# First attention's output projection as 24 products of high and low parts, with new orders of work on all engines

## The reference, cut to what matters

```python
x = x + attn(cond(x, cond_512, ...), norm_g, norm_b, Wq, Wkv, q_scale, k_scale, null_kv, Wout)
x = x + ffn(cond2(x, cond_512, ...), signatures_raw, knot_values, ..., norm_gamma, norm_beta, output_scale)

# in attn, for each sequence (n = 64, h = 16, dh = 64; two null keys in front)
out = jnp.einsum('bhij,bhjd->bhid', softmax(q @ k.T * 8 + bias), v)   # 64 x 1024 a sequence
out = out.transpose(0, 2, 1, 3).reshape(b, n, h * dh)
return out @ Wout                                                     # 1024 x 256
```

## Time and profile before

| | |
|---|---|
| median of 3 runs | 1833.0 us (1832.64 to 1834.09) |
| profiled execution, its own time | 1833.11 us |
| its span, first to last instruction | 1831.3 us |
| PE busy | 1718.0 us (94%) |
| DVE busy | 1545.9 us (84%) |
| ACT busy | 1198.5 us (65%) |
| POOL busy | 1173.0 us (64%) |
| mean granted TensorE clock | 0.970 |

### The profile page before, as it was taken

One profiled execution on the slowest core, in us unless ns is written; L12 is line 12 of the kernel. 1 busy time (PEld: TensorE's weight loads), 2 busy tenths in 40 slices (PEclk: granted clock), 3 DMA queues, 4 the chain that ended last, 5 costly groups with the idle time before them and its releaser, 6 DMA issues.

```text
span 1831.3 us, 62542 instructions
## 1 busy us (share of the span) xinstructions
PE 1718.0 (94%) x24806; PEld 1439.5 (79%) x24806; DVE 1545.9 (84%) x4182; ACT 1198.5 (65%) x2418; POOL 1173.0 (64%) x903
## 2 busy tenths in 40 slices
PE   4789999999999999999999999999999999999752
PEld 3568888888888888888888888888888888888641
DVE  5567799888989998889989988899899888998744
ACT  2456677777667777776676777676777777667431
POOL 0345557776777677767776777677767776776433
PEclk8899999999999999999999999999999999999875
DMA  4001222222222221222122212221222122212221
GB/s 150 15 9 29 42 49 49 49 55 59 48 46 53 59 49 45 53 59 49 45 56 56 52 42 55 56 52 45 55 54 55 43 52 55 55 47 50 55 54 44
DMA packets 341245, 93.63 MB, mean 51 GB/s; under 512 B 278289, under 2 KB 338097, under 8 KB 341169
## 3 DMA queue, kind: packets, MB, share of 16 engines
q1 hardware_dynamic: 338096, 82.04, 20.6%
q0 software_dynamic: 3072, 10.52, 2.1%
HBM read 58.95 MB, written 33.55 MB: 51 GB/s over the span
## 4 chain that ended last, share of the span: by engine, by line
PE 88%; DVE 5%; ACT 2%; POOL 1%; DMA 1%; issue 1%; SPq 1%; POOLq 0%; ACTq 0%; DVEq 0%
PE pa L442 29%; PE pb L421 7%; PE pa L449 6%; PE ps L645 6%; PE ps L487 6%; PE ps L472 5%; PE ps L479 4%; PE pc L542 4%; PE pc L622 3%; PE pa L421 3%; PE ps L557 3%; PE pb L433 3%; PE ps L489 2%; PE pb L551 2%; PE pb L428 2%; PE pc L568 1%
## 5 line engine op out<-in xcount | busy, mean ns | idle before, releaser
L1131 POOL TENSOR_TENSOR rn<-nrg,mhalf 128x16 f32<-128x16 f32 x64 | 186.6, 2915 | 160.6 <-DVE nrg L1037 160.6
L1117 POOL TENSOR_TENSOR rn<-nrg,mhalf 128x16 f32<-128x16 f32 x64 | 193.2, 3018 | 119.5 <-DVE nrg L970 119.4
L442 PE MATMUL pa<-wv,y 128*128 128x512 f32 x768 | 209.6, 409 | 0.0
L442 PE MATMUL pa<-wq,xnTs 128*128 128x512 f32 x768 | 205.1, 411 | 0.3 <-ACT kcat L703 0.3
L442 PE MATMUL pa<-wk,y 128*128 128x512 f32 x768 | 194.3, 402 | 0.9 <-ACT qn L722 0.9
L442 PEld LDWEIGHTS pa<-wq,xnTs 128*128 128x128 f32 x768 | 139.3, 191 | 51.8 <-issue 23.5
L442 PEld LDWEIGHTS pa<-wk,y 128*128 128x128 f32 x768 | 139.3, 188 | 30.9 <-ACT qn L722 1.7
L1111 POOL TENSOR_TENSOR pr<-pr,rden 128x1056 f32<-128x1056 f32 x64 | 124.7, 1949 | 54.5 <-DVE rden L943 51.8
L442 PEld LDWEIGHTS pa<-wv,y 128*128 128x128 f32 x768 | 135.4, 189 | 23.2
L1006 DVE TENSOR_TENSOR qn<-qn,rn 128x1024 f32<-128x1024 f32 x64 | 112.7, 1762 | 15.6 <-POOL rn L1117 15.0
L1092 POOL TENSOR_TENSOR kn<-kn,rn 128x1024 f32<-128x1024 f32 x64 | 122.0, 1905 | 5.0
(11 more groups left out here) (216 smaller groups left out, 4863.3 us busy)
## 6 DMA issues: line engine op xcount, KB each, us to landing
xT<-in_xT SPq DMA_DIRECT2D x64, 128.0 KB
x<-in_x SPq DMA_DIRECT2D x64, 128.0 KB, 2.1
kxdr<-kxn SPq DMA_DIRECT2D x64, 128.0 KB, 1.7
x1d<-x SPq DMA_DIRECT2D x64, 128.0 KB, 1.8
vm<-kxdr SPq DMA_DIRECT2D x128, 64.0 KB
odr<-o SPq DMA_DIRECT2D x256, 32.0 KB
on<-odr SPq DMA_DIRECT2D x64, 128.0 KB
xb<-x1d SPq DMA_DIRECT2D x64, 128.0 KB, 2.2
```

Source lines behind the costliest of these rows:

```text
L442: last = mm(bank, part(lhs(a_, k)), part(rhs(b_, k)), start=(n == 0), stop=(n == 3 * CK - 1))
L1117: g.tensor_tensor(rn[:, 0, :], nrg[:, 0, :], mhalf[:, :], ALU.pow).then_inc(S("q_rsqrt"), 1)
L1131: g.tensor_tensor(rn[:, 1, :], nrg[:, 1, :], mhalf[:, :], ALU.pow).then_inc(S("k_rsqrt"), 1)
```

## The change

The eight plain products become 24 in the rounded format. `wout2` holds the high and low parts of `Wout`, made once before the loop (a copy on ACT, a subtraction on DVE). ACT now copies the attention's output from PSUM to `oH` in the rounded format, and a new DVE operation a tile makes `oL`, PSUM minus `oH`. PE then does 16 products with `oH` and 8 with `oL`. The order within `step` is new on all five engines, the tiles' distances change with it (PE works at most 7 steps behind, where it was 9; SP writes the result 12 behind), and the last step index is `T + 11`. A few semaphores are merged or added (`v1_done`, `x1_done`, `k0_mm`, `oT_low`).

```diff
+        wout2 = sb("wout2", [P, 2, HP, C])
+        oH = sb("oH", [P, HP, P])
+        oL = sb("oL", [P, HP, P])
...
-            for i in range(last, T + 11):
+            for i in range(last, T + 12):
...
-                    for r in range(4, HP):
-                        mm(ps[:, 2, C:2 * C], oT[:, r, :], wout[:, r, :], start=False, stop=False)
...
+                if live(i, 3):
+                    wait(pe, "pr_add", t3)
+                if live(i, 4):
+                    for r in range(HP):
+                        for a in range(2):
+                            mm(ps[:, 2, C:2 * C], part(oH[:, r, :]), part(wout2[:, a, r, :]), start=(r == 0 and a == 0), stop=False)
...
+                if live(i, 4):
+                    for r in range(HP):
+                        mm(ps[:, 2, C:2 * C], part(oL[:, r, :]), part(wout2[:, 0, r, :]), start=False, stop=False)
...
-                if live(i, 4):
-                    for r in range(4):
-                        mm(ps[:, 2, C:2 * C], oT[:, r, :], wout[:, r, :], start=(r == 0), stop=False)
...
+            fn(part(wout2[:, 0, :, :]), wout[:, :, :], ACT.Copy).then_inc(S("high_parts"), 1)
...
+                if live(i, 4):
+                    wait(act, "pv_mm", t4)
+                    fn(part(oH[:, :, :].rearrange("p r (s l) -> p s r l", s=BT)),
+                       ps[:, 0:2, :].rearrange("p s (r l) -> p s r l", l=L), ACT.Copy).then_inc(S("oT_done"), 1)
...
+            dve.wait_ge(S("high_parts"), 4)
+            v.tensor_tensor(part(wout2[:, 1, :, :]), wout[:, :, :], wout2[:, 0, :, :], ALU.subtract)
...
+                if live(i, 4):
+                    wait(dve, "oT_done", t4)
+                    v.tensor_tensor(part(oL[:, :, :].rearrange("p r (s l) -> p s r l", s=BT)),
+                                    ps[:, 0:2, :].rearrange("p s (r l) -> p s r l", l=L),
+                                    oH[:, :, :].rearrange("p r (s l) -> p s r l", s=BT), ALU.subtract).then_inc(S("oT_low"), 1)
...
+                if live(i, 2):
+                    wait(pool, "k_rsqrt", t2)
+                    g.tensor_tensor(by_head(kn), by_head(kn), bc(rn[:, 1, :], 2, DH), ALU.mult).then_inc(S("kn_done"), 1)
+                if live(i, 3):
+                    wait(pool, "rden_done", t3)
+                    g.tensor_tensor(heads, heads, bc(rden[:, :], 2, J), ALU.mult).then_inc(S("pr_norm"), 1)
```

More of the change, by code:

```diff
@@ L338, in step @@
             def step(i, p):
[L339 to L360, removed]
+                t2, t4, t5, t6, t8, t10, t12 = i - 2, i - 4, i - 5, i - 6, i - 8, i - 10, i - 12
+                if live(i, 12):
+                    wait(sp, "res_done", t12)
+                    sp.dma_start(plain(out_t, t12), res[:, p, :]).then_inc(D("out", p), 16)
                 if live(i, 0):
@@ L501, in step @@
[L501 to L505, removed]
-                if live(i, 2):
[L507 to L511, removed]
@@ L581, in step @@
+                if live(i, 3):
                     for r in range(HP):
                         for t, s in ((0, 0), (1, 1), (1, 0), (0, 1)):
[L583 removed]
+                            last = pv_tile(r, t, s, 1 - p)
                     last.then_inc(S("pv_mm"), 1)
[L585 to L591 removed]
@@ L901, in step @@
-                if live(i, 9) or live(i, 10):
-                    if live(i, 10):
-                        wait(dve, "local_exp", t10)
-                    route = links_from(0, t9)
-                    route(v.tensor_scalar(fl[:, :, :], esc[:, :, :], 1.0, None, ALU.add))
-                    route(v.reciprocal(fl[:, :, :], fl[:, :, :]))
-                    route(v.scalar_tensor_tensor(out=over[:, :, :], in0=bc(both(fl), 2, KN), scalar=float(KN - 1),
-                                                 in1=bc(CO["steps"], 1, 2 * NC), op0=ALU.mult, op1=ALU.subtract))
@@ new lines, in step @@
+                if live(i, 7) or live(i, 8):
+                    if live(i, 8):
+                        wait(dve, "local_exp", t8)
+                    route = links_from(0, t7)
+                    route(v.tensor_scalar(fl[:, :, :], esc[:, :, :], 1.0, None, ALU.add))
+                    route(v.reciprocal(fl[:, :, :], fl[:, :, :]))
+                    route(v.scalar_tensor_tensor(out=over[:, :, :], in0=bc(both(fl), 2, KN), scalar=float(KN - 1),
+                                                 in1=bc(CO["steps"], 1, 2 * NC), op0=ALU.mult, op1=ALU.subtract))
@@ new lines, in step @@
+                if live(i, 7) or live(i, 8):
+                    route = links_from(3, t7)
+                    route(v.tensor_scalar(over[:, :, :], over[:, :, :], 0.0, 1.0, ALU.max, ALU.min))
+                    route(v.tensor_tensor(over[:, :, :], over[:, :, :], bc(rises[:, :], 1, 2 * NC), ALU.mult))
+                    route(v.tensor_reduce(both(gate), over[:, :, :], AX, ALU.add))
+                if live(i, 4):
+                    wait(dve, "x1T", t4)
+                    modulate(xm2, two(pb, 0), sty[:, 1, :, :], t4).then_inc(S("xm2_done"), 1)
@@ new lines, in step @@
+                if live(i, 8):
+                    v.scalar_tensor_tensor(out=slot[:, p:p + 1], in0=third[:, p, 0:1], scalar=float(TPC),
+                                           in1=third[:, 1 - p, 1:2], op0=ALU.mult, op1=ALU.add).then_inc(S("slot_done"), 1)
+                    wait(dve, "slot_done", t8)
+                    v.tensor_scalar(row[:, p, :], slot[:, p:p + 1], float(NT + TPC), None, ALU.add).then_inc(S("row_done"), 1)
+                if live(i, 6):
+                    wait(dve, "omT", t6)
+                    modulate(om, two(pb, 0), sty[:, 2, :, :], t6).then_inc(S("om_done"), 1)
```

744 lines of the change are left out of this document (378 added, 366 removed).

## The result

The changed kernel takes 2021.7 us (median of 4 runs, 2011.08 to 2029.41) against 1832.99 us for the kernel before (1832.64 to 1834.09), a ratio of 1.102 with a 95% interval of 1.097 to 1.108. It is slower by 189 us. The prediction said slower, by 128 us; the time lies above its range.

The account below looks back on a forecast made before the run. PE bounds the kernel at 26.11 us a step; DVE was to become the bound at 25.3 + 1.6 + 1.7 = 28.6. 1831.3 + 142 + 2.3 - 16, plus 1.8 around the span, makes 1961 us, range 1800 to 1995.

Parts of the forecast that it names:

- PE's part: PE's step: 26.11 less 3.46 for plain products plus 2.83 for 24 rounded ones, 25.5 us; new order counted at nothing.
- DVE's part: DVE's step: `oL` adds 1.15 us, `qn` loses 0.5 of blocking, 25.3 us; with both blocks 28.6, the new bound.
- the blocks: Two waits of DVE's routing operations for POOL products each step, beside `kn` and `pr`: 1.6 and 1.7 us.
- One-source scaling: Routing beside `kn`: blocked 1.4 us if the first two operations are free, up to 1.9; 1.6 taken.
- The first block: DVE's routing (`fl` twice and `over`) meets POOL's `kn`, just begun, and waits 1.6 us a step (1.4 to 1.9).
- Start and end: `wout`'s low part adds 2.3 us ahead of the first tile; smaller depth of PE takes off 16 us (0 to 30).
- The sum: 57 steps of 28.6 instead of 26.11 us add 142; with 2.3, -16 and 1.8 around the span, 1961 us.
- No block bites: Rival: both POOL products run beside free DVE work, PE sets a 25.7 us step, 1796 us; chance 0.23.
- One block: Rival: only one block, most likely the one beside `pr`, DVE's step 27.0 us, 1870 us; chance 0.13.
- the second block: DVE's second routing piece, behind the reciprocal, waits for POOL's product `pr` by `rden`: 1.7 us a step.
- The point from which a block decides: Block size on DVE below which its step stays under 26.11 us: 0.8 us.
- What would show it: Signs: step 28 to 29 us, DVE over 95% busy, L1003 to L1005 and L1019 lengthened, PE idle before L428, `oH` products 0.12 apart.

Follow-up runs that it names:

- the last version: Changed kernel with 85 more PE setup instructions and routing pieces 1 and 2 between the sum `den` and its reciprocal `rden`: 1794.47 us, also called the fastest version.
- the pair of runs: Changed kernel with 85 more PE instructions and routing pieces between `den` and `rden`, with the rounded format (1794.47 us) and with 8 plain products, no `oL` (1829.28 us).
- Two other versions without these blocks: Changed kernel with routing pieces 1 and 2 behind `pn`, 91 more PE instructions: 1863.86 us; with them behind `kxT`, 85 more: 1844.18 us.
- the run with the second block alone: Changed kernel with 85 more PE setup instructions and routing pieces 1 and 2 both directly behind the reciprocal `rden`: 1870.70 us.
- the run with the first alone: Changed kernel with 85 more PE setup instructions, routing piece 1 in its place behind `xnTs`, piece 2 behind `kxT`: 1833.66 us.
- the routing last: Changed kernel with 85 more PE setup instructions, routing piece 1 behind `kxT`, the rest at the end of DVE's step, POOL's gathering behind `rs`: 1872.18 us.
- behind `kxT`: Changed kernel with 85 more PE setup instructions and routing pieces 1 and 2 behind `kxT` on DVE: 1844.18 us.

## Why the prediction was right in direction and wrong in size

- **PE's part: right for the products, too low for the order.** The 16 `oH` products take 0.120 us each and the 8 `oL` ones 0.118, I took 0.118. PE's own step is at most the 25.89 us of the last version, 25.5 forecast. 8 x 0.216 x 2 less 24 x 0.118 was said to give 0.63 us; the pair of runs gives 26.49 - 25.89 = 0.60. But with plain products the last order takes PE 26.49 us, the kernel before 26.11. So a new order costs some 0.4 us a step, of which PE idles half (991 us busy of 1000 against 998), and I had counted it at nothing. In the changed kernel, where PE isn't the bound, that can't be read.
- **DVE's part: right.** `oL` took 1.22 us (1.22), `qn` 1.22, and the blocks 1.43 and 1.78 (1.6 and 1.7). With the refetching away the step is 28.73 us, forecast 28.6. DVE still waits some 0.6 us a step for PE there (19.9 us over 35 steps for `om`), so part of the agreement is luck: the ring in place of DVE work.
- **One-source scaling.** The first block was 1.43 us and not the upper 1.9, since the scaling of `fl` started ahead of `kn` and only L1005 was held by it. But the clamp that took 1.08 us beside `bd`, and 0.17 elsewhere, shows that a scaling of 16 elements is held as well.
- **Start and end: mis-sized.** The setup grew by 2.3 us, as forecast (first product 42.06 against 39.75). 57 x (28.73 - 26.11) + 2.3 = 152 us, but 120 were lost without the refetching, so start and end gave back 31 us, not 16, just beyond the bound I had given. (The same sum for the fastest version leaves 28.) I had put it down to the shorter depth, which no run changed by itself. The 52 steps behind its 12 tiles are counted over the 1358 us of the second window in the earlier trace rows.
- **The step that failed** is the one on PE's part that counts "its new order at nothing on PE itself", and with it the longer loop. The sum had no term for PE's program being fetched, 68 us. With the 68 that were measured, the forecast of 1961 would have been 2029, against 2021.7. The 8 us between 1961 and 1953.4 are two errors that partly cancel, 7 us too few for the steps and 15 too many for start and end. The trace of before showed the queue only where it cost nothing, and I didn't ask whether the loop's length or place mattered to it.
- **The rivals.** "No block bites" was given 1796 us. The last version, with no block on the routing and no refetching, takes 1794.5; that the numbers agree is partly luck, since its step is longer than the rival's 25.7 and its ends shorter. Two other versions without these blocks took 1863.9 and 1844.2, so blocks gone alone isn't enough. "One block" was given 1870: the run with the second block alone took 1870.7, but the run with the first alone 1833.7. The point from which a block decides isn't DVE's sum alone, it is where in the ring it lies.
- **"What would show it"** was right in three points: L1005 and L1019 lengthened, PE idle ahead of L428, products 0.12 us apart. DVE's busy share, 0.89 from 500 to 1500 us, was below the 95% I had named. A sign of being wrong was there too: DVE idle for over a microsecond, 4.1 to 5.1 us behind each of the 17 wraps with the wait.

## What to carry to other kernels

When a change makes a loop's program longer, look at the instruction queue inside the loop, before and after. Here idle time ended by "issue" at the same place of each pass (68.6 us at 17 wraps), together with packets there (9 a pass), meant that PE's loop was fetched again, and 91 instructions ahead of the loop cured it: 57 packets in all instead of 210, and 68 us less. Try small DVE operations with SBUF sources ahead of the one that starts POOL's product, not behind it, and in a place where DVE waits for PE anyway: L1005's work takes 0.29 us there and 1.72 beside `kn`. And where two engines each wait once a step for the other, add up the ring and not the engines: removing a block can bring less than it lasts (here 1.75 of 3.2 us a step), and moving work within the ring may bring nothing (here 1872.18 us with the routing last, 1844.18 with it behind `kxT`).

## What the runs showed of the hardware that I had not expected

- PE's loop of the kernel before (1576 instructions) had no packet of the instruction queue in any of the 23 passes behind its first wrap, in its own place and with 165 instructions more ahead of it (55 and 56 packets in all). With 205 more it had 8 to 10 packets in 20 of the 23 (236 in all). The changed kernel's loop (1614) had 9 in 17 of 23 (210 in all), and none with 91 more (57 in all). Every one of those 210 packets holds 16,384 bytes. With packets PE waited at a wrap, 68.6 / 17 = 4.0 us on average in the changed kernel and 119.9 / 20 = 6.0 in the kernel before with 205, and behind one such wait of the changed kernel the granted clock was 0.66 over 5 us.
- Waits that are already met weren't free on PE ahead of the first tile: 330 of them, two to an instruction, made the setup of the kernel before 57.52 - 39.75 = 17.8 us longer, 0.108 us for each of the 165 instructions.
- POOL's product held DVE's `SCALAR_TENSOR_TENSOR` (L1005, 1.72 us beside `kn`, 0.29 alone), `TENSOR_TENSOR` (L1019, 2.07 beside `pr`, 0.29 alone) and `TENSOR_SCALAR` (the clamp, 1.08 beside `bd`, 0.17 elsewhere), all with SBUF sources, to its end: they ended 0.03 to 0.15 us behind it. `RECIPROCAL` and the batch statistics, also with an SBUF source, ran at their usual 0.25 and 0.42 us inside such a product: in the changed kernel `fl`'s reciprocal, behind the start of `kn` at 999.30 (first row below), and in the fastest version DVE's statistics behind 1035.88 (the other rows; the scalings of `yT` are held again).

```profile
999.34 0.25 DVE L1004 RECIPROCAL fl<-fl 128x16 f32<-128x16 f32 x1
...
1035.88 1.96 POOL L1155 TENSOR_TENSOR pr<-pr,rden 128x1056 f32<-128x1056 f32 x1 [2.14 <-DVE rden L1023]
...
1036.09 0.42 DVE L1029 BATCH_NORM_STATS2 ys<-yy 128x6 f32<-128x256 f32 x1
...
1037.19 0.92 DVE L1038 TENSOR_SCALAR yT<-yT,cols 128x128 f32<-128x128 f32 x2
```
